# Four-block attention kernel: pair reductions for constant adds, moved visual sums and masks, and another order of probability transposes

## What is computed

```python
x = _L0_xattn_ref(x, ctx, ...)      # cross attention, weights quantised to three values
x = _L1_xattn_ref(x, ctx, mself, mcross, ...)  # masked self and cross attention, MLP with gelu, 3 layer norms
x = _L2_xattn_ref(x, ctx, ...)      # gated fusion with the pooled context
x = _L3_xattn_ref(x, ctx, mask, ...)  # RMS norm, grouped attention with rotary positions, gated MLP

# each attention of the first two blocks (16 heads of 8 features)
scores = einsum('bqhd,bkhd->bhqk', q, k) / sqrt(8)     # masked scores become a very negative number
probs = softmax(scores)
out = x + einsum('bhqk,bkhd->bqhd', probs, v) @ Wo     # the second block then layer-norms this sum
# layer norm: (x - mean) * rsqrt(var + 1e-5) * g + b;  RMS norm: x * rsqrt(mean(x^2) + 1e-6) * w
# L2: vision_pooled = mean(ctx over its 64 tokens), then two projections of it
# L2: weights = softmax(2 * agreement) over the tokens, after three iterations
```

## Time and profile before

| | |
|---|---|
| median of 3 runs | 496.73 us (496.45 to 497.52) |
| profiled execution, its own time | 496.65 us |
| its span, first to last instruction | 494.7 us |
| mean granted PE clock | 0.99 |
| PE busy | 445.4 us (90%), 6872 matmuls |
| DVE busy | 381.2 us (77%), 918 instructions |
| ACT busy | 299.3 us (60%) |
| POOL busy | 273.8 us (55%) |
| chain that ended last | PE 51%, DVE 24%, issue 14%, POOL 5%, ACT 4% |

### The profile page before, as it was taken

The page is one execution under the profiler, slowest core; times in us unless marked ns, Lnnn a source line. Parts: engine busy times, 40 slices in busy tenths (PEclk is TensorE's granted clock), DMA queues, the critical chain, the costliest instruction groups (busy, mean ns, idle before and its releaser), DMA issues.

```text
span 494.7 us, 16947 instructions
## 1 busy us (share of the span) xinstructions
PE 445.4 (90%) x6872; PEld 353.1 (71%) x6872; DVE 381.2 (77%) x918; ACT 299.3 (60%) x725; POOL 273.8 (55%) x332
## 2 busy tenths in 40 slices
PE   4698899999999999989989768999999999999876
PEld 4466666666666676679877656888888888878664
DVE  6699877688988888968889878877686876767632
ACT  2377676768676877666863655576656665544431
POOL 6464887579867787965644374454353535421210
PEclk9799999999999999999999999999999999999998
DMA  8960000000000000000000000000000000000000
GB/s 291 240 234 3 2 3 3 2 3 3 1 3 2 3 3 3 3 1 2 1 1 3 2 1 4 3 12 2 14 1 13 1 3 14 1 13 1 14 2 21
DMA packets 12421, 11.54 MB, mean 23 GB/s; under 512 B 5177, under 2 KB 10297, under 8 KB 12345
## 3 DMA queue, kind: packets, MB, share of 16 engines
q1 hardware_dynamic: 11624, 9.01, 6.7%
q10 hardware_dynamic: 720, 1.45, 0.8%
HBM read 9.42 MB, written 1.05 MB: 21 GB/s over the span
## 4 chain that ended last, share of the span: by engine, by line
PE 51%; DVE 24%; issue 14%; POOL 5%; ACT 4%; DMA 1%; DVEq 0%; POOLq 0%; ACTq 0%
DVE negm L1249 8%; PE ps L618 5%; DVE blocks L1240 5%; PE ps L634 4%; PE ps L656 4%; PE ps L448 4%; PE ps L734 4%; PE ps L466 3%; PE ps L532 2%; PE ps L545 2%; PE ps L611 2%; PE ps L626 2%; PE ps L496 2%; PE ps L664 2%; PE ps L408 2%
## 5 line engine op out<-in xcount | busy, mean ns | idle before, releaser
L1249 DVE TENSOR_REDUCE negm<-ps 128x8 bf16<-128x512 f32 x96 | 59.6, 683 | 24.9 <-PE ps L448 24.8
L833 ACT ACTIVATE p<-ps 128x512 f32<-128x512 f32 x96 | 54.7, 595 | 27.5 <-PE ps L456 26.4
L839 ACT ACTIVATE shared<-ps 128x512 f32<-128x512 f32 x96 | 57.0, 601 | 21.8 <-PE ps L466 20.4
L1742 POOL TENSOR_TENSOR wide<-wide,cv 128x1024 f32<-128x1024 f32 x24 | 45.5, 1896 | 32.8 <-ACT wide L823 32.8
L466 PE MATMUL ps<-cst,p 128*128 128x128 f32 x384 | 58.4, 276 | 0.4 <-ACT shared L839 0.4
L1795 POOL TENSOR_TENSOR probs<-p,rc 128x512 f32<-128x512 f32 x32 | 33.4, 1057 | 43.2 <-DVE rc L1535 43.1
L1669 POOL TENSOR_TENSOR rstd<-veps,neghalf 128x2 f32<-128x2 f32 x40 | 29.3, 732 | 46.4 <-DVE veps L1285 28.2
L466 PEld LDWEIGHTS ps<-cst,p 128*128 128x128 f32 x384 | 44.2, 141 | 11.5 <-issue 9.4
L1028 ACT ACTIVATE late<-ps 128x512 f32<-128x512 f32 x32 | 17.3, 594 | 34.3 <-PE ps L757 34.3
L618 PE MATMUL ps<-shared,wq 128*128 128x256 f32 x128 | 31.3, 386 | 5.2 <-ACT shared L976 3.4
L634 PE MATMUL ps<-wo,late 128*128 128x128 f32 x256 | 31.5, 276 | 4.0 <-ACT late L1028 3.8
(11 more groups left out here) (204 smaller groups left out, 1150.9 us busy)
## 6 DMA issues: line engine op xcount, KB each, us to landing
late<-in_mask_l SPq DMA_DIRECT2D x2, 512.0 KB, 11.0
result<-x_all SPq DMA_DIRECT2D x8, 128.0 KB, 1.8
x_all<-in_x_tok SPq DMA_DIRECT2D x1, 768.0 KB, 6.6
wide<-in_ctx_t SPq DMA_DIRECT2D x1, 768.0 KB, 8.1
rv<-in_rv ACTq DMA_DIRECT2D x1, 768.0 KB, 8.1
wa<-in_wa SPq DMA_DIRECT2D x1, 512.0 KB, 8.4
w<-in_w SPq DMA_DIRECT2D x2, 256.0 KB, 7.5
wq<-in_wq SPq DMA_DIRECT2D x1, 512.0 KB, 7.2
```

The lines of the kernel that those rows point to most:

```text
L833: A_(p3[:, n % 3, :], ps[:, S_BANK[r], :], ACT.Exp, scale=SC8).then_inc(sm["act_exp"], 1)
L839: A_(pt[:, w % 2, r, :], pt_bank(RG * w + r), ACT.Copy).then_inc(sm["act_pt"], 1)
L1249: V.tensor_reduce(negm[:, n % 4, :], ps[:, S_BANK[r], :].rearrange("p (a k) -> p a k", k=S), AX.X, ALU.max, negate=True).then_inc(sm["dve_ ...
L1742: P.tensor_tensor(r_op[:, w % 2, :, :], k_t[:, w % 2, :].unsqueeze(1).to_broadcast([128, 4, GT]), head_masks.unsqueeze(2).to_broadcast([12 ...
```

## The change

1. Every small DVE add of a constant becomes a `tensor_reduce` over a pair: the constant stands in a third (or second) column of the tile, written once at the start by four memsets, and the pair (variance, epsilon) is summed. The RMS squares get their 1/128 from ACT's own scale (0.088 before squaring), so that only the epsilon is left to add. The factor -2 is the negated sum of the same number twice.
2. The visual sum (128 x 2048 to 128 x 32) leaves pass 2 of DVE; its halves stand at the ends of passes 6 and 7. ACT's `vis_mean` moves from pass 5 to pass 8. The masks move from the end of pass 4 to the end of pass 5.
3. On PE bank 0's transposes stand between the second and the third subtraction, bank 1's ahead of `transposes_in`, bank 2's behind it and ahead of `project_out`. On ACT `evac_pt(w, 0)` stands between exps 1 and exps 2.

```diff
                 subtract_max(w, 1)
+                transpose_probs(w, 0)
                 subtract_max(w, 2)
                 subtract_max(w, 3)
-                transpose_probs(w, 0)
+                transpose_probs(w, 1)
                 if w + 2 < NW:
                     transposes_in(w + 2)
-                transpose_probs(w, 1)
                 if w in (VIS, VIS + 1):
                     pooled_visual(w - VIS)
+                transpose_probs(w, 2)
                 if older:
                     project_out(w - 2)
-                transpose_probs(w, 2)
...
                 exps(w, 0)
                 exps(w, 1)
+                evac_pt(w, 0)
                 exps(w, 2)
-                evac_pt(w, 0)
...
-                    A_(sq[:, i, :], x_all[:, TG * g + i, :], ACT.Square, accum_out=ss3[:, g % 2, i:i + 1]).then_inc(sm["h_sq"], 1)
+                    A_(sq[:, i, :], x_all[:, TG * g + i, :], ACT.Square, scale=RMS_SCALE, accum_out=ss3[:, g % 2, i, 0:1]).then_inc(sm["h_sq"], 1)
...
+            for eps, tile in ((LN_EPS, mv[:, :, :, 2]), (LN_EPS, mv2[:, :, :, 2]), (RMS_EPS, ss3[:, :, :, 1]),
+                              (RMS_EPS, ssm[:, :, :, 1])):
+                V.memset(tile, eps).then_inc(sm["eps_set"], 1)
+            dve.wait_ge(sm["eps_set"], 4)
             dve.wait_ge(sm["ld_w0"], 16)
...
-                V.tensor_scalar(veps[:, g % 2, :], mv[:, g % 2, :, 1], LN_EPS, None, ALU.add).then_inc(sm["ln0_ve"], 1)
+                V.tensor_reduce(veps[:, g % 2, :], mv[:, g % 2, :, 1:3], AX.X, ALU.add).then_inc(sm["ln0_ve"], 1)
...
+            def visual_sums(i):
+                if i == 0:
+                    dve.wait_ge(sm["ld_ctx0"], 16)
+                    dve.wait_ge(sm["ld_ctx"], 16)
+                b = slice(i * B // 2, (i + 1) * B // 2)
+                V.tensor_reduce(vpool[:, b], ctx_t[:, :].rearrange("p (b k) -> p b k", k=S)[:, b, :], AX.X, ALU.add)\
+                    .then_inc(sm["v_sum"], 1)
...
-                V.tensor_scalar(veps[:, gs, :], mv[:, gs, :, 1], LN_EPS, None, ALU.add).then_inc(sm[s + "ve"], 1)
+                V.tensor_reduce(veps[:, gs, :], mv[:, gs, :, 1:3], AX.X, ALU.add).then_inc(sm[s + "ve"], 1)
...
-                if w == 2:
-                    dve.wait_ge(sm["ld_ctx0"], 16)
-                    dve.wait_ge(sm["ld_ctx"], 16)
-                    V.tensor_reduce(vpool[:, :], ctx_t[:, :].rearrange("p (b k) -> p b k", k=S), AX.X, ALU.add)\
-                        .then_inc(sm["v_sum"], 1)
-                if w == 4:
+                if w == 5:
                     masks()
+                if w in (6, 7):
+                    visual_sums(w - 6)
...
-                V.tensor_scalar(agm2[:, gs, :], agm[:, gs, :], -2.0, None, ALU.mult).then_inc(sm["g_max2"], 1)
+                V.tensor_reduce(agm2[:, gs, :], agm[:, gs, :].unsqueeze(2).to_broadcast([128, GB, 2]), AX.X, ALU.add, negate=True).then_inc(sm["g_max2"], 1)
...
-                V.tensor_scalar(msm[:, g % 2, :], ssm[:, g % 2, :], 1.0 / D, RMS_EPS, ALU.mult, ALU.add)\
+                V.tensor_reduce(msm[:, g % 2, :], ssm[:, g % 2, :, :], AX.X, ALU.add)\
```

More of the change, by code:

```diff
@@ L39 @@
 LN_EPS, RMS_EPS, Q_EPS = 1e-5, 1e-6, 1e-5
+RMS_SCALE = D ** -0.5
 SC8 = float(DH) ** -0.5
@@ L157, in build @@
         st = sb("st", [128, 2, TG, 6])
-        mv = sb("mv", [128, 2, TG, 2])
+        mv = sb("mv", [128, 2, TG, 3])
         veps = sb("veps", [128, 2, TG])
@@ L187, in build @@
         st2 = sb("st2", [128, 2, TG, 6])
-        mv2 = sb("mv2", [128, 2, TG, 2])
+        mv2 = sb("mv2", [128, 2, TG, 3])
         veps2 = sb("veps2", [128, 2, TG])
@@ L196, in build @@
         first_exp = sb("first_exp", [128, 1])
-        ss3 = sb("ss3", [128, 2, TG])
+        ss3 = sb("ss3", [128, 2, TG, 2])
         ms3 = sb("ms3", [128, 2, TG])
@@ L216, in build @@
         sqm = y[:, 0, :, :]
-        ssm = sb("ssm", [128, 2, TG])
+        ssm = sb("ssm", [128, 2, TG, 2])
         msm = sb("msm", [128, 2, TG])
@@ L235, in row @@
             return rv[:, RV[name], :].unsqueeze(1).to_broadcast([128, n, D])
-        names = """ld_x0 ld_x ld_small ld_cst ld_bv ld_rv ld_w0 ld_wa ld_ctx0 ld_ctx ld_w ld_m ld_w3 cst_bf quant q_sum q_abs q_gam q_gc ones_set pz
+        names = """ld_x0 ld_x ld_small ld_cst ld_bv ld_rv ld_w0 ld_wa ld_ctx0 ld_ctx ld_w ld_m ld_w3 cst_bf quant q_sum q_abs q_gam q_gc ones_set eps_set pz
             ln0_mv ln0_ve ln0_r ln0 m_bias m3_split
@@ L845, in vis_mean @@
             def vis_mean():
-                act.wait_ge(sm["v_sum"], 1)
+                act.wait_ge(sm["v_sum"], 2)
                 A_(vmean[:, :], vpool[:, :], ACT.Copy, scale=1.0 / S).then_inc(sm["v_mean"], 1)
@@ L885, in _ @@
                     cast_selectors()
-                if w == 5:
+                if w == VIS:
                     vis_mean()
@@ L951, in m_sq @@
                         act.wait_ge(sm["m_sq"], n - 1)
-                    A_(sqm[:, i % 2, :], x_all[:, n, :], ACT.Square, accum_out=ssm[:, g % 2, i:i + 1]).then_inc(sm["m_sq"], 1)
+                    A_(sqm[:, i % 2, :], x_all[:, n, :], ACT.Square, scale=RMS_SCALE, accum_out=ssm[:, g % 2, i, 0:1]).then_inc(sm["m_sq"], 1)
             def rms(g):
@@ L1181, in ln0 @@
                     dve.wait_ge(sm["ln0_mv"], 4 * g + 1 + t)
-                    V.bn_aggr(mv[:, g % 2, t, :], st[:, g % 2, t, :]).then_inc(sm["ln0_mv"], 1)
+                    V.bn_aggr(mv[:, g % 2, t, 0:2], st[:, g % 2, t, :]).then_inc(sm["ln0_mv"], 1)
                 dve.wait_ge(sm["ln0_mv"], 4 * g + 4)
-                V.tensor_scalar(veps[:, g % 2, :], mv[:, g % 2, :, 1], LN_EPS, None, ALU.add).then_inc(sm["ln0_ve"], 1)
+                V.tensor_reduce(veps[:, g % 2, :], mv[:, g % 2, :, 1:3], AX.X, ALU.add).then_inc(sm["ln0_ve"], 1)
             def scales():
@@ L1282, in layer_norm @@
                     dve.wait_ge(sm[s + "st"], TG * n + t + 1)
-                    V.bn_aggr(mv[:, gs, t, :], st[:, gs, t, :]).then_inc(sm[s + "mv"], 1)
+                    V.bn_aggr(mv[:, gs, t, 0:2], st[:, gs, t, :]).then_inc(sm[s + "mv"], 1)
                 dve.wait_ge(sm[s + "mv"], TG * n + TG)
-                V.tensor_scalar(veps[:, gs, :], mv[:, gs, :, 1], LN_EPS, None, ALU.add).then_inc(sm[s + "ve"], 1)
+                V.tensor_reduce(veps[:, gs, :], mv[:, gs, :, 1:3], AX.X, ALU.add).then_inc(sm[s + "ve"], 1)
             def residual(w):
@@ L1453, in rms_mean @@
                 dve.wait_ge(sm["h_sq"], TG * g + TG)
-                V.tensor_scalar(ms3[:, g % 2, :], ss3[:, g % 2, :], 1.0 / D, RMS_EPS, ALU.mult, ALU.add)\
+                V.tensor_reduce(ms3[:, g % 2, :], ss3[:, g % 2, :, :], AX.X, ALU.add)\
                     .then_inc(sm["h_ms"], 1)
```

## The result

| | before | after |
|---|---|---|
| median | 496.67 us (4 runs, 496.45 to 497.52) | 492.69 us (4 runs, 491.88 to 493.52) |
| profiled execution, span | 496.65, 494.7 us | 491.88, 490.0 us |
| DVE waits for scores, L1249 / L1262 | 24.8 us, 18 times | 20.7 us, 20 times |
| passes 8 to 12 | 8.16 to 8.25 us | 7.92 us |
| passes 13, 14, 15 | 8.89, 8.16, 8.89 | 7.92, 7.92, 7.71 |

What follows compares the result with a forecast made beforehand. PE was taken to set the pace in 18 of 24 passes, with late DVE or POOL lengthening others. Reduces -1.44, order -2.56 and passes 0 to 5 +0.17 gave -3.83: 496.65 to 492.8 us, range 489.8 to 495.9.

Steps and rivals of the forecast that it cites:

- Adds by tensor_reduce: Small DVE adds: POOL no longer holds veps in passes 13 and 15, 0.72 us each, -1.44 in all.
- the sentence that takes two places for the whole: No other veps of the 32 took longer than those in passes 13 and 15: 0 more, bound -1.0 us.
- Order: On PE, Q and K start 5.28 instead of 5.44 us into a pass: -0.16 each, -2.56 over 16 passes.
- Rivals 1: ACT's exp 2, started later, holds up PE's bank 2 transposes: 0.32 us lost a pass, 500.5 us; chance 0.09.
- Rival 2: PE's changes between subtraction and transposes, or a wait of 0.32, eat the order's gain: 495.4 us; chance 0.17.
- Visual sum: On DVE, pass 3 starts 1.28 us earlier; the halves behind passes 6 and 7 fit DVE's idle: 0.
- Masks: End of pass 5 on DVE: masks held by POOL's mask_k until about 67.12; passes 0 to 5 together +0.17 us.
- rival 3: Masks in pass 5 not held by mask_k: pass 6 starts 1.27 us earlier, 491.5 us; chance 0.08.
- rival 4: POOL's cast, 0.40 us, goes first between the two mask instructions: 493.2 us; chance 0.07.
- Memsets: Four DVE memsets before the first reduce fit a DVE idle of 2.82 us: 0.
- rival 5: Starting DVE memsets wait for POOL's widest fill; first reduce at 4.4 us, not 3.80: 493.4 us; chance 0.05.

Runs made afterwards that it cites:

- Experiment 4: The changed kernel with one line put back, the second block's veps a tensor_scalar again: 498.97 us.
- experiment 7: The changed kernel with ACT's list as before (exps 2 ahead of evac_pt 0), PE's list still changed: 497.63 us.
- experiment 8: The changed kernel with the masks back at the end of pass 4, all else as changed: 490.09 us.
- experiment 9: The changed kernel with the masks split, the first in pass 7 and the second in pass 8: 489.53 us, run again 488.88 us.
- experiment 1: The kernel before with only the new PE and ACT order: 496.55 us.
- experiment 2: The kernel before with only the visual sum and the masks moved: 498.57 us.

## Why the prediction was right, and where it was not

The total was right: 492.8 forecast, 492.69 measured. That it came within 0.1 us is in part luck, as the steps show. Against the trace, from pass 0 to 23 (first trace; second in brackets):

| step | forecast | measured |
|---|---|---|
| passes 0 to 5 | +0.17 | +0.78 (+0.41) |
| pass 6 | -0.16 | +0.91 (+0.97) |
| passes 7 to 21 | -3.84 | -5.47 (-5.49) |
| pass 22 | 0 | -0.25 (-0.25) |
| sum | -3.83 | -4.03 (-4.36) |

- **Adds by tensor_reduce, -1.44.** No reduce was held, and the two passes lost their surplus: 1.67 where the reduces stand alone, since pass 15 has a base of 7.95, not 8.17. What failed is the sentence that takes two places for the whole: they were counted in the old order. Experiment 4 gives 6.9 in the new one. The sum survived because both were changed together. By its terms the order alone would have made 494.1; it measured 496.55.
- **Order, -0.16 a pass.** Bank 2's transposes started at S+4.25 (4.26 forecast), released by exp 2 as worked out. The term was mis-sized at the end: bank 2's transposes and `project_out` were taken to hold PE for 1.02; it was 0.95 (119.20 to 120.15), and Q and K came at S+5.20 instead of 5.28. So 0.24 a pass, 1.3 more in 16 passes; passes 8 and 9, 8.25 before, gained 0.33. Pass 22, forecast to end by DVE, gained 0.25 as well. Rivals 1 and 2 fell. Rival 2's price, a wait of 0.32 that eats the gain, shows in experiment 7: 0.36 on PE, though for the copy and not for exp 2.
- **Visual sum.** Pass 2 was to get 1.28 + 0.16 shorter; it got 1.52 (8.90 to 7.38). The halves took 1.20 each; the maxima behind them still waited for PE (0.43 and 0.82 us): hidden, as forecast.
- **Masks, +0.17 with the rest of passes 0 to 5.** The first was held as forecast, until 66.09 against 66.01 for `mask_k`, so rival 3 fell. From the residual's start to S of pass 6 they took 2.56 (64.26 to 66.82); the forecast had 2.36 (65.51 to 67.87). The second mask took 0.88 against the 0.69 and 0.67 of experiments 8 and 9, with POOL's cast begun 0.06 ahead of it: rival 4 in a small form, 0.2. In the first trace pass 1 lost 0.36, which the second didn't show.
- **The clock: the step that was not there.** The text had no term for what PE's idle of 3.32 us in pass 5 leaves behind. Pass 6 lasts 8.52 and 8.58, against 7.27 in experiment 8: 1.3 us, about what the order gave beyond forecast.
- **Memsets, 0.** They ran from 0.93 us on in 0.06 and 0.07 each, and qs began at 3.69: hidden, rival 5 fell.

So the right total holds two errors of about 1.3 us of opposite sign (pass 6's clock against the order's size), and the attribution to parts was wrong where two of them meet.

## What to carry to other kernels

Before a reordering, list how far each short instruction of one engine starts ahead of the long one of the other engine that can hold it, and take the shift off. What decides is which of the two starts first: 0.32 us less 0.24 left 0.07 here, and that held until one late pass turned it round; then it stayed turned. So look at the latest pass, not only at the usual one. Two edits of which one removes what the other runs into must be tried together as well as apart. Beside the moved work (498.57), the reduces alone make 495.98, the order with veps as a tensor_scalar 498.97, both 492.05: -2.6 (1.4 of it in the passes), +0.4 and -6.5 us. Put work that can be held where its engine idles and the neighbour is free, and look at what a long stop does to PE's clock behind it.

## What the runs showed of the hardware

- **A hold can keep itself up.** 0.10 us decide: veps 0.07 before `mask_k` takes 0.17, veps 0.03 behind it 1.89, and this repeats for eight passes in experiment 1 and seven in 4. The Trainium skill (SBUF — State Buffer, Who interferes with whom) says that whoever starts first has the port pair for its whole instruction; these rows agree. The same section keeps tensor_reduce out of it on trn2. The changed kernel's 32 veps of 156 to 159 ns agree, among them those of passes 13 to 15, which start 0.47 us or more behind `mask_k`'s start.
- **A tensor_tensor of DVE is held as well**: `a_tok`, 0.98 instead of 0.42, with POOL's add 0.04 us ahead (experiment 4). The Trainium skill (same section) says that a DVE instruction with two inputs in SBUF contends with a GpSimd one that reads SBUF; `o_t` and `rden` are two such inputs, and the row agrees. The prediction did not look at the late `a_tok` of passes 13 and 15; in every trace it stands ahead of the first veps that `mask_k` holds, and without it that veps would start ahead of `mask_k`.
- **So is a tensor_scalar from int32 to bf16**: the first mask takes 1.33 and 1.49 us beside `mask_k`, 0.21 and 0.23 without it (with: experiment 2 and the changed kernel; without: experiment 9 and the kernel before).
- **Half clock behind a long stop, but not always.** In the seven profiled executions in which pass 5 lasts 10.7 to 10.8 us, with PE idle for 2.9 to 3.3 at its end, pass 6 lasts over 8.5 and has stretches at a granted clock of 0.5 to 0.8; with the masks elsewhere (7.3 to 7.6) it doesn't. Yet stops of the same length go either way. PE's idle of 3.17 us near 285 us is followed by half clock in the changed kernel and not in the kernel before:

```profile
282.43 0.41 PE L612 MATMUL ps<-cst,fus 128*128 128x128 f32 x2 [3.17 <-POOL fus L1846]
...
283.53 1.97 PE L735 MATMUL ps<-wide,blocks 64*64 64x64 f32 x64
```

```profile
286.64 0.41 PE L611 MATMUL ps<-cst,fus 128*128 128x128 f32 x2 [3.17 <-POOL fus L1836]
...
287.73 1.16 PE L734 MATMUL ps<-wide,blocks 64*64 64x64 f32 x64
```

The order alone had half clock from 61 to 65 us behind a stop of 1.79 us, while experiment 8 has a stop of 1.77 us in the same place and keeps 1.00 (the order alone, then experiment 8):

```profile
60.64 0.39 PE L456 MATMUL ps<-negm,idb 128*128 128x512 bf16 x1 [1.79 <-DVE negm L1249]
60.96 1.81 PE L480 MATMUL ps<-shared,blocks 128*32 128x64 f32 x64
```

```profile
59.23 0.39 PE L457 MATMUL ps<-negm,idb 128*128 128x512 bf16 x1 [1.77 <-DVE negm L1262]
59.54 1.10 PE L481 MATMUL ps<-shared,blocks 128*32 128x64 f32 x64
```

What tells these cases apart no run here shows. It goes with much of the scatter: the kernel before, timed beside the experiments, took 493.2 to 494.3 us at a mean granted clock of 1.00, 496.1 to 497.1 at 0.990 and 497.6 to 498.3 at 0.986. A difference of 1 to 2 us between medians is therefore read from the passes too.
